# Layers: sums of squares of two head groups in one group of products, joined by a maximum, the squares in buffers of their own

## The reference, cut to what matters

```python
def l2norm(t):
    return t / jnp.maximum(jnp.linalg.norm(t, axis=-1, keepdims=True), 1e-12)

def attn_layer(x, Wqkv, qs, ksc, Wo):          # DEPTH = 6, HEADS = 16, DIM_HEAD = 64, WINDOW = 32
    qkv = x @ Wqkv
    q, k, v = jnp.split(qkv, 3, -1)
    ...
    q = l2norm(q) * qs
    k = l2norm(k) * ksc
    ...                                         # rotary tables on q and k
    out = local_attention(q, k, v)
    return out @ Wo
...
for i in range(DEPTH):
    x = attn_layer(shift_tokens(x), Wqkv[i], q_scale[i], k_scale[i], Wo[i]) + x
    x = ffn_layer(shift_tokens(x), ln_g[i], ln_b[i], W1[i], b1[i], W2[i], b2[i]) + x
```

## Time and profile before

| | |
|---|---|
| time, median of 3 executions | 2510.15 us (2502.93 to 2514.1) |
| profiled execution, first to last instruction | 2515.4 us |
| PE, matmul | 2362.9 us busy (94%) |
| DVE | 1744.7 us busy (69%) |
| ACT | 1598.6 us busy (64%) |
| POOL | 1463.1 us busy (58%) |
| mean granted clock of PE | 0.971 |

### The profile page before, as it was taken

One profiled execution on the slowest core, in us unless ns is written; L12 is line 12 of the kernel. 1 busy time (PEld: TensorE's weight loads), 2 busy tenths in 40 slices (PEclk: granted clock), 3 DMA queues, 4 the chain that ended last, 5 costly groups with the idle time before them and its releaser, 6 DMA issues.

```text
span 2515.4 us, 122084 instructions
## 1 busy us (share of the span) xinstructions
PE 2362.9 (94%) x53677; PEld 1738.9 (69%) x53677; DVE 1744.7 (69%) x3537; ACT 1598.6 (64%) x5036; POOL 1463.1 (58%) x1408
## 2 busy tenths in 40 slices
PE   9958999999999999999999999999878999999967
PEld 8836777777777777777777777777645666666657
DVE  4477888888878888878787888887335555555534
ACT  3226777777777787777777877777625444545422
POOL 1166667656666667666666677665117656566307
PEclk9979999999999999999999999999979999999978
DMA  4013333333333334333333343333216222222136
GB/s 91 15 33 86 85 78 96 95 80 85 93 88 94 81 83 103 92 83 81 88 95 85 79 97 82 84 92 84 57 22 185 48 48 48 48 48 48 30 95 250
DMA packets 230210, 204.62 MB, mean 81 GB/s; under 512 B 133687, under 2 KB 155464, under 8 KB 229552
## 3 DMA queue, kind: packets, MB, share of 16 engines
q1 hardware_dynamic: 225296, 190.91, 30.6%
q0 software_dynamic: 2208, 5.58, 0.6%
q10 hardware_dynamic: 2176, 0.33, 0.1%
HBM read 86.05 MB, written 15.70 MB: 40 GB/s over the span
## 4 chain that ended last, share of the span: by engine, by line
PE 72%; DVE 17%; issue 4%; SPq 2%; ACT 2%; DMA 1%; POOL 1%; POOLq 0%; ACTq 0%; DVEq 0%
PE psum L1208 8%; PE psum L1226 6%; PE psum L1955 5%; PE psum L1234 5%; PE psum L1109 5%; PE psum L1934 5%; PE psum L1940 4%; PE psum L1111 4%; PE psum L1110 3%; DVE kT L1443 3%; PE psum L1989 3%; PE psum L1979 3%; DVE rotated L1418 3%; PE psum L1185 2%; PE psum L1216 2%
## 5 line engine op out<-in xcount | busy, mean ns | idle before, releaser
L1354 ACT ACTIVATE p<-p,stat 128x64 f32<-128x64 f32 x1536 | 512.5, 336 | 40.1 <-DVE stat L1490 38.0
L1573 POOL TENSOR_TENSOR p<-p,inverse 128x512 f32<-128x512 f32 x192 | 200.2, 1043 | 465.9 <-DVE inverse L1493 464.9
L1208 PE MATMUL psum<-kT,qT 32*32 32x64 f32 x24576 | 306.7, 223 | 30.3 <-issue 29.1
L2088 DVE TENSOR_REDUCE largest<-psum 128x1 f32<-128x512 f32 x256 | 165.0, 686 | 228.0 <-PE psum L1940 228.0
L1208 PEld LDWEIGHTS psum<-kT,qT 32*32 32x32 f32 x24576 | 264.0, 103 | 82.2 <-issue 81.1
L1354 ACT ACTIVATION_READ_ACCUMULATOR p<-p,stat 128x1 f32 x1536 | 288.6, 188 | 0.0
L1418 DVE SCALAR_TENSOR_TENSOR rotated<-psum,scales,rotary 128x512 f32<-128x512 f32 x384 | 271.1, 742 | 24.3 <-ACT sq L1290 24.2
L1552 POOL TENSOR_TENSOR sq<-sq 128x512 f32<-128x512 f32 x192 | 245.1, 1276 | 42.4 <-ACT sq L1290 42.1
L1290 ACT ACTIVATE sq<-psum 128x512 f32<-128x512 f32 x384 | 212.8, 581 | 63.3 <-PE psum L1139 45.9
L1226 PEld LDWEIGHTS psum<-pT,v_win 64*64 64x64 f32 x12288 | 197.3, 135 | 47.6 <-issue 40.6
L1109 PE MATMUL psum<-xs,wqkv_high 128*128 128x512 f32 x384 | 204.9, 534 | 24.3 <-DVE rotated L1418 24.3
(11 more groups left out here) (352 smaller groups left out, 5448.6 us busy)
## 6 DMA issues: line engine op xcount, KB each, us to landing
v_win<-v_tok SPq DMA_DIRECT2D x576, 128.0 KB
rnorm_wide<-rnorms SPq DMA_DIRECT2D x384, 64.0 KB
v_win<-v_tok SPq DMA_DIRECT2D x336, 64.0 KB
q_rows<-q_rows_all SPq DMA_DIRECT2D x32, 512.0 KB, 4.6
tile_weights<-expert_table SPq DMA_DIRECT2D x23, 512.0 KB, 6.1
wqkv<-L_ffn_Wqkv SPq DMA_DIRECT2D x96, 64.0 KB, 2.4
rel_values<-sq SPq DMA_DIRECT2D x60, 64.0 KB, 2.2
wo<-L_ffn_Wo SPq DMA_DIRECT2D x48, 64.0 KB
```

Of the source, the lines that this page charges most:

```text
L1208: last = PE.e.matmul(psum[WIN * blk:WIN * (blk + 1), f, out], q[rows, g, half, tok:tok + WIN], k[rows, g, half, tok:tok + 2 * WIN], start= ...
L1354: last = A.e.activation(p, p, ACT.Exp, bias=t.stat[:, h, 2 * g + f:2 * g + f + 1], accum_out=t.sum[:, h, g, f:f + 1])
L1573: G.e.tensor_tensor(p, p, t.inv[:, h, :, :].unsqueeze(3).to_broadcast([P, GROUPS_TF, 2, 2 * WIN]), ALU.mult).then_inc(*t.p_scaled.by(m))
```

## The change

The squares of piece p go into a new buffer `sq_both[p % 2]` instead of in place. PE no longer sums after each piece: after the odd ones it issues eight products, four for piece p - 1 and four for piece p, that accumulate into the same four places of one ring bank. DVE takes, instead of the copy or addition, the maximum of the result with `least` (first pair of a kind) or with the norms so far (second pair); the maximum L1434 ahead of the inverse root is gone. ACT waits for `squares` ahead of both halves. POOL additionally waits for the sums that last read the buffer it writes.

```diff
@@ transformer_setup
+    t.sq_both = [sb(f"squares{i}", [P, S]) for i in range(2)]
-    t.made, t.squares, t.summed, t.counted = (per(n, units, pairs) for n in ("made", "squares", "summed", "counted"))
+    t.made, t.squares = (per(n, units, pairs) for n in ("made", "squares"))
+    t.summed, t.counted = (per(n, units, pairs[1::2]) for n in ("summed", "counted"))
@@ ring_takes, and the same condition in unit_tensor
-    if SUM_LAG <= s < SUM_LAG + UNIT and (s - SUM_LAG) % 4 == 0:
+    if SUM_LAG <= s < SUM_LAG + UNIT and (s - SUM_LAG) % 8 == 4:
@@ unit_tensor
         PE.wait_ge(*t.squares.on((u, p)))
-        for k in range(TPB):
-            last = PE.e.matmul(ps[32 * k:32 * k + 32, 0:P], t.onehot[:, kind * GROUPS_TF + g, :], t.sq[0][:, k * P:(k + 1) * P], start=True, stop=True)
+        for x in (p - 1, p):
+            kind, g, lo = piece(x)
+            for k in range(TPB):
+                last = PE.e.matmul(ps[32 * k:32 * k + 32, 0:P], t.onehot[:, kind * GROUPS_TF + g, :], t.sq_both[x % 2][:, k * P:(k + 1) * P], start=(x < p), stop=(x == p))
@@ unit_scalar
-                A.wait_ge(*(t.squares if half else t.summed).on((u, p - 1) if p else (u - 1, 2 * GROUPS_TF - 1)))
+                A.wait_ge(*t.squares.on((u, p - 1) if p else (u - 1, 2 * GROUPS_TF - 1)))
@@ unit_vector
-    if 0 <= p < 2 * GROUPS_TF and at == 0:
+    if 0 <= p < 2 * GROUPS_TF and at == 0 and p % 2:
-        kind, first = divmod(p, GROUPS_TF)
+        kind, second = p // GROUPS_TF, p % GROUPS_TF > 1
+        x = t.norms[kind][:, :]
         V.wait_ge(*t.summed.on((u, p)))
-        if first:
-            V.wait_ge(*t.counted.on((u, p - 1)))
-            V.e.tensor_tensor(t.norms[kind][:, :], t.norms[kind][:, :], ps, ALU.add).then_inc(*t.counted.by((u, p)))
-        else:
-            V.e.tensor_copy(t.norms[kind][:, :], ps).then_inc(*t.counted.by((u, p)))
+        if second:
+            V.wait_ge(*t.counted.on((u, p - 2)))
+        V.e.tensor_tensor(x, ps, x if second else t.least[:, 0:1].to_broadcast([P, P]), ALU.max).then_inc(*t.counted.by((u, p)))
@@ unit_vector, ahead of inverse_root
-            V.e.tensor_tensor(x, x, t.least[:, 0:1].to_broadcast([P, P]), ALU.max).then_inc(*own.up())
@@ unit_gpsimd
-        G.e.tensor_tensor(t.sq[0][:, :], t.sq[0][:, :], t.sq[1][:, :], ALU.add).then_inc(*t.squares.by((u, p)))
+        if u or p >= 2:
+            before = p - 1 - p % 2
+            G.wait_ge(*t.summed.on((u, before) if before > 0 else (u - 1, 2 * GROUPS_TF - 1)))
+        G.e.tensor_tensor(t.sq_both[p % 2][:, :], t.sq[0][:, :], t.sq[1][:, :], ALU.add).then_inc(*t.squares.by((u, p)))
```

More of the change, by code:

```diff
@@ L1132, in unit_tensor @@
         three_products(PE, psum[:, 4 + at, :], w, xs).then_inc(*t.projected.by((u, (p, at))))
-    if SUM_LAG <= s < SUM_LAG + UNIT and (s - SUM_LAG) % 4 == 0:
+    if SUM_LAG <= s < SUM_LAG + UNIT and (s - SUM_LAG) % 8 == 4:
         p = (s - SUM_LAG) // 4
-        kind, g, lo = piece(p)
         ps = ring_take(c, t, "unit", u, f"sum{p}")
         PE.wait_ge(*t.squares.on((u, p)))
-        for k in range(TPB):
-            last = PE.e.matmul(ps[32 * k:32 * k + 32, 0:P], t.onehot[:, kind * GROUPS_TF + g, :], t.sq[0][:, k * P:(k + 1) * P], start=True, stop=True)
+        for x in (p - 1, p):
+            kind, g, lo = piece(x)
+            for k in range(TPB):
+                last = PE.e.matmul(ps[32 * k:32 * k + 32, 0:P], t.onehot[:, kind * GROUPS_TF + g, :], t.sq_both[x % 2][:, k * P:(k + 1) * P], start=(x < p), stop=(x == p))
         last.then_inc(*t.summed.by((u, p)))
```

## The result

The changed kernel takes 2494.4 us (median of 6, 2487.95 to 2506.73) where the kernel before takes 2511.61 us (median of 6, 2502.93 to 2514.37): ratio 0.9929, 95% interval 0.9906 to 0.9952, 17 us or 0.7% faster. Run again with its variants, beside another series of the kernel before, it gave 0.9925 (0.9898 to 0.9952).

A forecast was written before the change was run, and what follows sets the result against it. PE was taken to bound all but a 17 us stretch per unit set by DVE. Per unit 0.40 (DVE) + 0.42 + 0.12 - 0.11 (PE) = 0.83 us, 19.1 us over 23 units, from 2510.15 to 2491 us; range 2480 to 2506.

The forecast's parts named there:

- the DVE half: DVE ahead of the inverse root of the queries' norms: removing the maximum there saves 0.40 us a unit.
- Two rounds more cost 0.22 us: PE's sum over two pieces: two added rounds cost 0.22 us; a pair saves 0.14, with ends of 0 and 0.17.
- The ring's 0.12 us: First sum of a unit on PE, late because its ring bank waits for DVE; removed, saving 0.12 us.
- L217 takes over L1434's wait; 0.40 us saved, not 1.16: DVE at the queries' inverse root: L217 inherits the wait for POOL once L1434 is gone; 0.40 us a unit saved.
- The L1427 of piece 6 counts nothing: DVE's sum between two L1443 on the chain: its removal counts 0, with 0.20 us as the other end.
- No wait grows on PE: Ring waits on PE: 4 fewer users a unit let each look back at an older one, so none grows.
- issue: PE held by its own instructions, 25.3 us at L1208: a quarter of the 0.42 given back, 0.11 us a unit.
- What remains at the turn, 0.6 us: Turn after the mix: 0.87 - 0.40 + 0.14, about 0.6 us a unit, is left of DVE's stretch.
- Passing to the end: PE sets the end outside DVE's stretch, so three of four pairs count: 3 x 0.14 = 0.42 us a unit.
- the PE half: PE's sums in pairs and the ring, less what is given back: 0.42 + 0.12 - 0.11 us a unit.
- only one half comes: Rival: PE's gain is lost, 2498 us, or DVE's 0.40 us is lost to POOL, 2500 us; chance 0.24.
- The slower rival, one collision more: Rival: DVE's chain waits for one more POOL operation in every unit, 0.16 us a unit longer, 2514 us; chance 0.07.

The follow-up runs named there:

- the second profile: Profile of the changed kernel, unedited, run again beside its own variants; ratio 0.9925 to the kernel before.
- the pairs alone: Changed kernel, but DVE still copies the first sum, adds the second and takes the maximum ahead of the root: 2506.03 us against 2516.36, ratio 0.9958.
- the maximum alone: Kernel before, PE summing piece by piece in place, but DVE joins each sum by a maximum, none ahead of the root: 2500.54 us against 2516.36, ratio 0.9930.
- The sums twice: Changed kernel with every pair's eight products issued twice: 2528.34 us against the kernel before's 2516.36, ratio 1.0038.
- the buffers alone: Kernel before with squares in the two new buffers and ACT not waiting for PE's sum; PE sums piece by piece, DVE as before: ratio 0.9994.
- the later root: Inverse root of the queries' norms one step later, behind the inverse of the softmax sums: ratio 1.0281 in the kernel before, 1.0065 in the changed kernel.

## Why the prediction was right, and where it was not

Forecast 2491 us, 19.1 us a run; measured 2494.4 us, 17 us, inside the range and beyond its interval from no change. A unit took 68.19 us (67.64 in the second profile), forecast 67.9. The two mechanisms are the forecast ones; that the total fits is in part luck, since the DVE half is too small in it and a wait of PE that took a part of the joint gain is missing. By its own steps:

- **Two rounds more cost 0.22 us.** Measured 0.574 - 0.356 = 0.218 us, so 0.14 us a pair. The longer runs on the same tiles were the right measure, and neither end was needed. Over a unit, PE's time from the start of a sum to the next instruction's fell from 2.85 to 2.32 us (2.30 with the pairs alone): 0.53, where four pairs at 0.14 make 0.56.
- **The ring's 0.12 us.** It came. In the kernel before one sum a unit started 0.41 to 0.46 us behind the start of L1111, the others 0.32 or 0.33; after, none starts later than 0.33. At one place a unit where a sum is gone the products with the values now start 0.38 us behind that L1113 and not the 0.32 counted, 0.06 us that the sum did not have.
- **L217 takes over L1434's wait; 0.40 us saved, not 1.16.** Shown by the changed kernel and by the maximum alone: L217 lasts 1.05 us, and ends 0.15 us after POOL's instruction. The rule of the Trainium skill that was weighed there (SBUF — State Buffer, "Summary: rules for kernel authors") agrees with both. From the last count to the inverse the median is 4.55 us (1334.05 to 1338.60 in the chain), where it was 4.95; forecast were 4.5 and 4.88. On average over the 23 units the saving was 0.39 us (5.03 to 4.64), and 0.31 with the maximum alone (4.72).
- **The L1427 of piece 6 counts nothing.** Open. With the pairs alone, where L1434 stays, the distance from mix to turn fell by 0.19 us, but for the greater part because the mix came later (the pairs alone, above). From the scaling of the keys ahead of this L1427 to the one behind it the mean is 1.82 us before, 1.67 with the pairs alone, and 1.83 and 1.68 in the two profiles of the changed kernel. Between 0 and the 0.20 of the other end the profiles do not decide.
- **No wait grows on PE.** This step failed. The ring argument was right in itself, the second value product waits for the same copy as before. But that copy waits for DMA, which did not come sooner when PE did: ACT sat idle for it 27.7 us in all, where it was 17.5. The place went from 0.67 to 1.01 us on average (0.83 in the second profile), 0.16 to 0.34 us a unit. The wait reaches the turn: in the changed kernel the turn came 19.7 us behind the mix before in the 8 of 22 units where the place took over 0.7 us, and 18.4 us in the 14 others (second profile: 19.1 in 7 and 18.0 in 15). With the pairs alone it was 19.6 us in 13 units and 18.4 in 9, in the kernel before 18.9 in 4 and 18.6 in 18. The sum let "issue" take back 0.11 us a unit, and that was too little and the wrong wait. Idle time put down to "issue" ahead of the scores did not grow: 25.3 us before, 22.2 us after.
- **What remains at the turn, 0.6 us.** It was 2.24 - 1.80 = 0.44 us. In the 14 units without that wait it was 2.34 - 1.80 = 0.54 us, near the forecast, in the 8 with it 0.31, since there the mix comes late.
- **Passing to the end.** The sums twice agree with three groups of the four costing their time and the fourth being hidden, within an interval of some 7 us.
- **The two halves are not two terms.** The maximum alone gives 0.9930, the pairs alone 0.9958, the two together 0.9925 to 0.9929, not the 0.9888 of the product. In the sum the DVE half was 9 us and the PE half 10. The pairs came out at 10.6; the maximum alone at 17.6, with an interval that leaves 9 out. Together they add little to the maximum alone. The wait behind L1180 goes the right way, since the maximum alone takes only 0.75 us there, but it has not been shown to be the whole. Why the maximum alone gains twice its term stays open: its units are 0.56 us shorter than before, as much as two profiles of the changed kernel differ from one another (0.55), and those of the buffers alone are 0.31 us shorter in their profile with no gain in time, so one profile cannot say. So the total was right, with the DVE half too small and the joint gain too large.

Of the rivals, "only one half comes" is not what happened: each half alone brought its own gain, 10.6 and 17.6 us, and the eight products cost 0.574 us and not the 0.71 of two groups. But the two together gain hardly more than the maximum alone. The slower rival, one collision more, did not occur in the change; the later root shows what it is like, with L222 long as well.

## What to carry to other kernels

Small products on column tiles cost a fixed amount for each group as well as one for each round: here 0.14 us and 0.109 us, so joining groups pays even when the number of products stays. When an instruction is taken out that is long because it waits for another engine, look at the next one of the same operands: it inherits the wait, and only the unwaited length is won. And before moving an instruction out of a chain, ask what it was running beside: the inverse root looked like 5 us of delay but 1.3 us of it filled a wait for ACT, and what stood behind it in DVE's order was awaited too. One step in the order cost 2.8%, and about half of that came with a lower clock of PE: when an edit brings new waits to a busy PE, compare the granted clock before pricing the waits.

## What the runs showed that I had not expected

The chain of waits names one cause at each step, and so hides the next one. In the kernel before it put the turn down to the root; the later root brought the turn 0.45 us nearer to the mix, and waits of PE for two other results of DVE that cost more. Two edits of one number each in the order of steps, both meant to shorten a measured wait of under 1 us a unit and both doing so, cost 2 to 3% (ratios 1.0281 and 1.0239 on the kernel before). And the clock: a single idle stretch of PE of 2.83 us was followed by 4 us at a mean granted clock of 0.57. A shorter one stood ahead of another fall: in the changed kernel's profile PE was busy for 0.90 us of the 2 us from 498 us on, its longest idle time there being 1.10 us, and from 500 to 503.3 us it was granted 0.50.
